# Spreading two of five expert blocks' scores by DMA and weighing them on GpSimd

## The chip, the cores and the metric

The kernel runs on one core of one Trainium2 chip. The metric is the device time of one execution in microseconds; the median of several executions is compared. Matmuls run on TensorE (PE), elementwise work on VectorE (DVE), ScalarE (ACT) and GpSimd (POOL); SyncE (SP) issues DMAs.

## What is computed

64 images of 64x64 pixels with 3 channels go through a Fourier tower of four layers (a small forward transform, a mix of the modes, an inverse transform, a 1x1 convolution, GELU) and a head of two layers, which leaves one 64x64 image each. These are read as 64 sequences of 64 tokens with 64 features, 4096 tokens in all. Then come a retention block, and a layer of 64 experts of which each token uses the best 6. The last is what the change is about:

```python
logits = jnp.einsum('bsd,ed->bse', x, gate_w)
top_logits, indices = jax.lax.top_k(logits, TOP_K)
scores = jax.nn.softmax(top_logits, axis=-1)
W_sel = lattice_weights[indices]
xW = jnp.einsum('bsd,bskde->bske', x, W_sel)
lattice_out = jnp.einsum('bske,bsk->bse', xW, scores)
proj = jnp.einsum('bsd,ed->bse', lattice_out, out_w) + out_b
```

The projection is normalised over the features, scaled, and added to the input of the expert layer.

## The kernel before

The kernel has two blocks, `tower` and then `transformer`. The transformer handles the tokens in 4 chunks (CHUNKS) of 1024 tokens (SLOT), and has two stages.

The first, which I call the front of the transformer, follows an order written out by hand in the list `FRONT`: turns (transposes on PE), projections, retention, gate logits. Each step fills one of four PSUM slots of 1024 columns, and ACT or DVE moves it out; a step may start when the slot that it reuses is moved out. The last steps of a chunk are the gate, its top 6 (`rank`, `take`, `softmax` on DVE, `exponent` on ACT), and `s_turn`, which turns the scores so that experts lie on partitions and tokens along the row (`halves_t`, each score split into a rounded part and the rest, 64 + 64 partitions).

The second, the expert stage, computes every expert for every token, and weighs it by its score, which is zero for the experts not chosen. Two experts make a block (64 features each fill the 128 partitions), so there are EB = 32 blocks a chunk and 128 in all. A block N = 32 g + n takes three steps:

- `spread_block` on PE (L1056): two matmuls of 512 columns with a 0/1 matrix `select` copy the two experts' score rows onto 64 partitions each, into one of PB = 3 PSUM slots.
- `weigh_half` on DVE (L1268), twice: spread scores times `y_t`, the turned tokens (doubled to 128 partitions), into one of WB = 4 buffers `weighted`.
- `gather` on PE (L1067): two matmuls in f32 with the experts' weights add the block to a PSUM sum for the chunk.

On PE the spreads of two blocks stand ahead of the gathers of the two before them. When the 32 blocks of a chunk are summed, ACT copies the sum, PE multiplies it with `out_w` (`project`, L1083), and DVE normalises it in nine steps, `finish(g, 0)` to `finish(g, 8)`. These stand between the weighings of the next chunk, one after each second block from n = 8 to n = 24; the last chunk's nine steps end the kernel. GpSimd prepares two sums for each chunk (L1507, L1509), and SP stores the results (L955).

Much scratch lies in the tower's large tile, so the profile calls `y_t`, `weighted`, `h` and others by the name `modes`.

Of the kernel before, what the change touches and what calls it, by code (L numbers as in the profile page):

```python
# [9 lines left out]
F32 = mybir.dt.float32  # L10
# [29 lines left out]
CT = TILES // CHUNKS  # L40
WB = 4
H_STORES = 8 * 16
# [115 lines left out]
class Front:  # L158

    def __init__(self, ctx, nc):  # L160
        self.modes = ctx.enter_context(nc.sbuf_tensor("modes", [128, IMAGES, MODES // 2, 32], F32))
        self.space, self.at = flat(self.modes[:]), 0
        self.h = self.part(TILES, D)
        self.centred_x = self.part(CHUNKS, CT, D)
        self.normed = self.part(CHUNKS, CT, D)
        self.stats_x = self.part(CHUNKS, 3, CT)
        self.w = self.part(3 * D)[0:D]
        self.rope = self.part(4, D)
        self.decay = self.part(128)
        self.y_t = self.part(TOKENS)  # L170
        self.y2 = self.part(TILES, 2, D)
        self.weighted = self.part(WB, SLOT)
# [629 lines left out]
class Steps:  # L802
# [28 lines left out]
    ("qkv", 3, 1), ("y_turn", 1, 0), ("scores", 2, 0), ("gate", 1, 0), ("attend", 2, 0), ("qk_turn", 3, 0),  # L831
    ("qk_turn", 3, 1), ("s_turn", 0, 0), ("scores", 3, 0), ("y_turn", 2, 0), ("attend", 3, 0), ("gate", 2, 0),
    ("s_turn", 1, 0), ("y_turn", 3, 0), ("gate", 3, 0), ("s_turn", 2, 0), ("s_turn", 3, 0)
])
GUARD = 3.0e38
EB = EXPERTS // 2
PB = 3


def transformer(nc, slots, ident, front, h_dram, gate_t, lattice, out_wt, out_b, ln_g, ln_b, k_select, out):  # L840

    with ExitStack() as ctx:
# [8 lines left out]
        w, rope, decay = front.w, front.rope, front.decay  # L851
        y_t, y2, weighted = front.y_t, front.y2, front.weighted
        h_stored, h_in, front_in, x_variance = front.h_stored, front.h_in, front.front_in, front.x_variance
# [6 lines left out]
        turned = sb("at_turned", [128, 2, 2, CT, D])  # L860
        qk_t = weighted[0:D].rearrange("p (b q) n -> p b q n", q=2)
# [43 lines left out]
        weigh = sem("ex_weigh")  # L905
        summed = sem("ex_summed")
        mixed_out = sem("ex_mixed_out")
# [15 lines left out]

        def after_weigh(g, n, half):

            return 2 * (g * EB + n) + half + 1

        @block.sync
        def _(sp):
# [21 lines left out]
            for c in range(2, CHUNKS):  # L951
                load_select(c)
            for g in range(CHUNKS):
                sp.wait_ge(result_set, g + 1)
                sp.dma_start(out.rearrange("(t b) h w -> (b h) t w", b=2)[:, tiles_of(g)],  # L955
                             result[:, g % 2]).then_inc(stored[g % 2], 16)
            for b in range(2):
                sp.wait_ge(stored[b], 16 * CHUNKS // 2)

        @block.tensor  # L960
        def _(pe):
# [85 lines left out]

            def spread_block(g, n):

                for half in range(2):  # L1050
                    N = g * EB + n
                    if N >= PB:

                        pe.wait_ge(weigh, 2 * (N - PB) + half + 1)
                    at = g * SLOT + half * 512
                    nc.tensor.matmul(slots[:, N % PB, half * 512:(half + 1) * 512],  # L1056
                                     select[:, n * 128:(n + 1) * 128], halves_t[:, at:at + 512],
                                     start=True, stop=True).then_inc(spread, 1)

            def gather(g, n):  # L1060

                pe.wait_ge(weigh, after_weigh(g, n, 1))
                if n == 0 and g >= 2:

                    pe.wait_ge(added, g - 1)
                for j in range(2):
                    mm = nc.tensor.matmul(slots[j * D:(j + 1) * D, SLOTS - 1, g % 2 * 512:g % 2 * 512 + 512],  # L1067
                                          lattice_w[:, n, :],
                                          weighted[:, (g * EB + n) % WB, j * 512:(j + 1) * 512],
                                          start=(n == 0), stop=(n == EB - 1))  # L1070
                if n == EB - 1:
                    mm.then_inc(summed, 1)

# [44 lines left out]
            qk_turn(3, 1)  # L1118
            s_turn(0)
            score(3)  # L1120
            y_turn(2)
            attend(3)
            gate(2)
            s_turn(1)
            y_turn(3)
            gate(3)
            s_turn(2)
            s_turn(3)

            pe.wait_ge(weights_in, WEIGHTS)  # L1130
            wait_moved("s_turn", CHUNKS - 1)
# [3 lines left out]
            spread_block(0, 0)  # L1135
            spread_block(0, 1)
            for g in range(CHUNKS):
                for k in range(EB // 2):
                    for n in (2 * k + 2, 2 * k + 3):
                        if n < EB:  # L1140
                            spread_block(g, n)
                        elif g + 1 < CHUNKS:
                            spread_block(g + 1, n - EB)
                    for n in (2 * k, 2 * k + 1):
                        gather(g, n)
                    if k == 1 and g > 0:
                        project(g - 1)
            project(CHUNKS - 1)
# [4 lines left out]
        def _(dve):  # L1153
# [78 lines left out]
            def rank(c):  # L1232

                wait_moved("gate", c)
                for t in range(CT):
                    last = nc.vector.max(top[:, t, :], logits[:, c % 2, t, 0:EXPERTS])  # L1236
                link(last)
                nc.vector.tensor_tensor(level[:, c % 2], logits[:, c % 2, :, 0:EXPERTS], along(top[:, :, 0], EXPERTS),
                                        ALU.subtract).then_inc(shifted, 1)
# [22 lines left out]

            def weigh_half(g, n, half):

                N = g * EB + n
                dve.wait_ge(spread, after_weigh(g, n, half))
                at = g * SLOT + half * 512
                nc.vector.tensor_tensor(weighted[:, N % WB, half * 512:(half + 1) * 512],  # L1268
                                        slots[:, N % PB, half * 512:(half + 1) * 512], y_t[:, at:at + 512],
                                        ALU.mult).then_inc(weigh, 1)  # L1270
# [83 lines left out]
            wait_moved("s_turn", CHUNKS - 1)  # L1354
            for g in range(CHUNKS):
                for n in range(EB):
                    for half in range(2):
                        weigh_half(g, n, half)
                    if g > 0 and n >= 8 and n % 2 == 0 and n // 2 - 4 < 9:
                        finish(g - 1, n // 2 - 4)  # L1360
            for step in range(9):
# [3 lines left out]
        def _(act):  # L1365
# [51 lines left out]
            def move_s(c):  # L1417

                move("s_turn", c, 0, halves_t[:, c * SLOT:(c + 1) * SLOT])

            def round_select(c):

# [41 lines left out]
            round_select(3)  # L1464
            move_s(0)
            double_y(2)
            move_y(2)
            move_gate(2)
            root_y(3)
            move_s(1)  # L1470
            exponent(2)
            double_y(3)
            move_y(3)
            move_gate(3)
            move_s(2)
            exponent(3)
            move_s(3)
            for g in range(CHUNKS):
                act.wait_ge(summed, g + 1)
# [3 lines left out]
                root(nc, stats_o[:]).then_inc(o_root, 1)  # L1483

        @block.gpsimd
        def _(pool):
# [15 lines left out]
            pool.wait_ge(weights_in, WEIGHTS)  # L1502
            for g in range(CHUNKS):
                pool.wait_ge(y_set, g + 1)
                if g >= 2:
# [4 lines left out]
                                        ALU.add).then_inc(h_shifted, 1)  # L1510


def build(nc, x, x_turned, fc0, fc0_t, sw, cwt, cb, fc1_w, fc1_b, fc2_w, fc2_b, wqkv, gate_t, lattice,
          out_wt, out_b, ln_g, ln_b, k_fwd_w, k_fwd_h, k_inv_h, k_inv_w, k_lift_mask,
          k_rope, k_decay, k_select,
          k_ident, out):
    h_dram = nc.dram_tensor("h_scratch", (IMAGES, HH, WW), F32, kind="Internal").ap()
    with (
        nc.psum_tensor("slots", [128, SLOTS, SLOT], F32) as slots,
# [8 lines left out]
              k_fwd_w, k_fwd_h, k_inv_h, k_inv_w, k_lift_mask)  # L1528
        transformer(nc, slots, ident, front, h_dram, gate_t, lattice, out_wt, out_b, ln_g, ln_b, k_select, out)

# [54 lines left out]
```

## Time and profile before

| | |
|---|---|
| median of 3 runs | 1771.46 us (1771.33 to 1779.39) |
| profiled execution | 1771.06 us, of which its span is 1769.3 us |
| PE busy | 1631.4 us (92%) |
| DVE busy | 1246.6 us (70%) |
| ACT busy | 581.4 us (33%) |
| POOL busy | 28.9 us (2%) |
| expert stage, first spread to last gather | 1553.4 to 1755.6 us |

The span goes from the first to the last instruction; 1.8 us of the execution lie outside of it. The whole change lies behind 1518 us of the span. A `L` number is a line of the kernel before; an f32 matmul of one line of code appears as two in the profile.

### The profile page before, as it was taken

To read this page: it belongs to the slowest core of one execution; us is meant where nothing else is said; L and a number is where in the kernel's file an instruction comes from. 1 tells how busy PE (TensorE), PEld (TensorE's weight loads), DVE (VectorE), ACT (ScalarE), POOL (GpSimd) and SP (SyncE) were. 2 spreads that over 40 slices of the span, in tenths; PEclk is the share of its full clock that TensorE was granted. 3 is DMA by queue.
4 is the path that set the end of the run, shared out by engine and by line. 5 is a ranking of instruction groups with operands and counts; after the bars stand their busy time and mean duration, and the time that the engine had idled before them with its cause. 6 is when DMAs were issued, how large, how long until landed. Compare 5 with 4: busy or idle time off the path is not lost. (4 is left out here: it accounts for less than half of the span.)

```text
span 1769.3 us, 43294 instructions
## 1 busy us (share of the span) xinstructions
PE 1631.4 (92%) x19696; PEld 949.9 (54%) x19696; DVE 1246.6 (70%) x1500; ACT 581.4 (33%) x779; POOL 28.9 (2%) x21
## 2 busy tenths in 40 slices
PE   7999999989999999899999989999988868699997
PEld 2665555557555555665555548777611128534432
DVE  3398988966898898588988974555300028878887
ACT  2333223223232232132322313444478855300000
POOL 1000000000000000000000000000000003000000
PEclk9999999999999999999999999999999988689998
DMA  5233232245655655456556553999876630000000
GB/s 194 81 139 123 118 144 98 119 182 170 241 208 230 231 209 233 143 215 232 209 229 232 208 206 109 335 359 356 330 272 232 231 113 24 1 1 1 7 6 12
DMA packets 59222, 300.01 MB, mean 170 GB/s; under 512 B 17504, under 2 KB 19488, under 8 KB 25120
## 3 DMA queue, kind: packets, MB, share of 16 engines
q1 hardware_dynamic: 40608, 163.01, 27.0%
q10 hardware_dynamic: 18432, 134.23, 18.4%
q8 instruction: 156, 2.56, 0.6%
q14 instruction: 26, 0.21, 0.0%
HBM read 160.90 MB, written 136.31 MB: 168 GB/s over the span
## 5 line engine op out<-in xcount | busy, mean ns | idle before, releaser
L519 PEld LDWEIGHTS slots<-inv_w,inv_out 128*128 128x128 f32 x4096 | 499.1, 196 | 179.3 <-issue 179.3
L756 ACT ACTIVATE act_c<-slots,conv_b 128x512 f32<-128x512 f32 x512 | 352.2, 688 | 739.6 <-PE slots L519 739.6
L519 PE MATMUL slots<-inv_w,inv_out 128*128 128x128 f32 x4096 | 540.7, 287 | 0.0
L673 DVE STREAM_TRANSPOSE inv_out<-slots 128x1024 f32<-128x1024 f32 x256 | 304.6, 1228 | 98.3 <-PE slots L491 98.3
L649 DVE STREAM_TRANSPOSE turned_h<-slots 128x1024 f32<-128x1024 f32 x200 | 237.9, 1228 | 37.4 <-PE slots L429 37.0
L638 DVE STREAM_TRANSPOSE turned_w<-act_c 128x1024 f32<-128x1024 f32 x192 | 225.2, 1216 | 0.0
L429 PE MATMUL slots<-turned_w,fwd_w 32*64 32x512 f32 x3200 | 202.7, 615 | 17.9 <-DVE turned_h L649 10.4
L1268 DVE TENSOR_TENSOR modes<-slots,modes 128x512 f32<-128x512 f32 x256 | 158.4, 683 | 27.2 <-PE slots L1056 25.7
L767 ACT ACTIVATE inv_out<-slots,b 128x1024 f32<-128x1024 f32 x128 | 135.6, 1110 | 25.1 <-PE slots L599 25.1
L441 PE MATMUL slots<-turned_h,fwd_h 64*64 64x320 f32 x1600 | 138.2, 458 | 4.9 <-DVE modes L655 4.9
L655 DVE STREAM_TRANSPOSE modes<-slots 128x640 f32<-128x640 f32 x96 | 81.4, 847 | 86.5 <-PE slots L441 86.5
L511 PE MATMUL slots<-act_c,conv_w 32*32 32x512 f32 x3072 | 111.7, 604 | 19.9 <-DVE modes L655 15.0
L1067 PE MATMUL slots<-modes,ex_lattice_w 128*64 128x512 f32 x512 | 126.4, 610 | 0.1
L491 PE MATMUL slots<-turned_k,inv_h 32*64 32x320 f32 x2048 | 102.1, 454 | 13.5 <-DVE turned_k L663 7.2
L429 PEld LDWEIGHTS slots<-turned_w,fwd_w 32*64 32x64 f32 x3200 | 60.4, 133 | 86.6 <-issue 68.3
L663 DVE STREAM_TRANSPOSE turned_k<-modes 128x640 f32<-128x640 f32 x128 | 103.1, 808 | 0.1
L599 PE MATMUL slots<-act_c,w 32*64 32x512 f32 x1024 | 73.3, 626 | 22.7 <-ACT inv_out L767 20.2
L478 PE MATMUL slots<-modes,mode_w 64*64 64x128 f32 x1600 | 90.3, 270 | 3.8 <-DVE modes L655 2.9
L478 PEld LDWEIGHTS slots<-modes,mode_w 64*64 64x64 f32 x1600 | 89.3, 132 | 6.2 <-DVE modes L655 4.7
L728 DVE TENSOR_SCALAR turned_h<-slots,b 128x512 f32<-128x512 f32 x4 | 3.0, 751 | 118.4 <-PE slots L610 118.4
L441 PEld LDWEIGHTS slots<-turned_h,fwd_h 64*64 64x64 f32 x1600 | 52.0, 133 | 54.0 <-issue 11.0
L695 DVE COPY modes<-slots 128x640 f32<-128x640 f32 x40 | 33.0, 825 | 67.2 <-PE slots L478 67.2
(121 smaller groups left out, 806.3 us busy)
## 6 DMA issues: line engine op xcount, KB each, us to landing
act_scratch<-act_c ACTq DMA_DIRECT2D x128, 1024.0 KB, 4.8
act_c<-act_scratch SPq DMA_DIRECT2D x128, 1024.0 KB, 5.1
mode_w<-in_sw_dram SPq DMA_DIRECT2D x40, 320.0 KB, 3.0
turned_w<-in_x_turned_dram SPq DMA_DIRECT2D x4, 1024.0 KB, 5.6
xin<-in_x_dram SPq DMA_DIRECT2D x4, 1024.0 KB, 7.5
ex_select_raw<-in_k_select_dram SPq DMA_DIRECT2D x4, 512.0 KB, 4.2
h_scratch<-turned_h SPq DMA_DIRECT2D x32, 32.0 KB, 3.1
modes<-h_scratch SPq DMA_DIRECT2D x8, 128.0 KB, 4.6
```

The lines of the kernel that those rows point to most:

```text
L429: mm = nc.tensor.matmul(banks[i * 64:(i + 1) * 64, 4 + p, :], fwd_w[p * 32:(p + 1) * 32, wh, :], turned_w[p * 32:(p + 1) * 32, n % 2, wh, ...
L441: mm = nc.tensor.matmul(banks[kwh * 64:(kwh + 1) * 64, i, 0:320], fwd_h[i * 64:(i + 1) * 64, parity, ph, :], turned_h[i * 64:(i + 1) * 64, ...
L478: mm = nc.tensor.matmul(mix_sums(rows_b, k)[:, at:at + 128], mode_w[rows_b, n % RING_W, m, :], modes[rows_b, :, k, 2 * m:2 * m + 2], start ...
L511: nc.tensor.matmul(banks[q * 32:(q + 1) * 32, p, :], w, src, start=True, stop=False, skip_group_check=True)
L519: mm = nc.tensor.matmul(banks[:, p, at:at + 128], inv_out[:, t % 2, i, p, :, :, r].rearrange("p b o -> p (b o)"), inv_w[:, i, :], start=Fa ...
L638: last = nc.vector.transpose(dst, src)
L649: nc.vector.transpose(dst, src).then_inc(w_turned, 1)
L673: nc.vector.transpose(dst, src).then_inc(inv_turned, 1)
L756: nc.scalar.activation(act_c[:, t % RING, :, p, :], banks[:, p, :].rearrange("p (i m) -> p i m", i=2), ACT.Gelu, bias=conv_b[:, l:l + 1]). ...
L767: nc.scalar.activation(unit[:, n % 2, a:a + 2, :], banks[:, at:at + 2, :], ACT.Gelu, bias=b1[:, 0:1]).then_inc(unit_set, 1)
L1067: mm = nc.tensor.matmul(slots[j * D:(j + 1) * D, SLOTS - 1, g % 2 * 512:g % 2 * 512 + 512], lattice_w[:, n, :], weighted[:, (g * EB + n) % ...
L1268: nc.vector.tensor_tensor(weighted[:, N % WB, half * 512:(half + 1) * 512], slots[:, N % PB, half * 512:(half + 1) * 512], y_t[:, at:at + ...
```

## The change

Of every five blocks N, those with N % 5 of 1 or 3 are now weighed on GpSimd: 51 of 128. Their scores are not spread by PE. A new turn, `level_turn`, follows each `s_turn` in the front and turns the unsplit scores; ACT moves them into `level_t` (64 partitions, one for each expert), SP stores them into a DRAM tensor `level_dram`, and for each GpSimd block SP loads two of its rows, each repeated onto 64 partitions, into one of six buffers `rows_of` (ROWS_RING) made of front tiles that are free by then. GpSimd multiplies the whole 128x1024 block at once. `weighted` gets six buffers, and a semaphore `gathered` counts the blocks that PE has summed, since both writers must wait for a buffer to be read. The stores of the result move from SP's queue to ACT's.

```diff
-WB = 4
+WB = 6
...
+ROWS_RING = 6
+def on_pool(N):
+
+    return N % 5 in (1, 3)
...
+        weighted = [front.weighted[:, b, :] for b in range(4)]
+        weighted += [flat(qkv[:])[:, 2 * SLOT:3 * SLOT], flat(centred_y[:])]
+        rows_of = [flat(turned[:])[:, 0:SLOT], flat(turned[:])[:, SLOT:2 * SLOT], flat(ret_t[:])[:, 0:SLOT],
+                   flat(ret_t[:])[:, SLOT:2 * SLOT], flat(straight[:]), flat(crossed[:])]
+        level_t = normed_t
...
+            e, n = FRONT.moved_of("attend", CHUNKS - 1)
+            sp.wait_ge(moved[e], n)
+            for c in range(CHUNKS):
+                e, n = FRONT.moved_of("level_turn", c)
+                sp.wait_ge(moved[e], n)
+                sp.dma_start(level_dram[:, c * SLOT:(c + 1) * SLOT], level_t[:, c % 2, :]).then_inc(level_stored[c], 16)
+            for i, N in enumerate(POOL_BLOCKS):
+                g, n = N // EB, N % EB
+                if i >= ROWS_RING:
+                    sp.wait_ge(weigh_pool, i - ROWS_RING + 1)
...
+                sp.wait_ge(level_stored[g], 16)
+                sp.dma_start(rows_of[i % ROWS_RING], level_dram[2 * n:2 * n + 2, g * SLOT:(g + 1) * SLOT].rearrange(
+                    "e (a t) -> e a t", a=1).broadcast_to([2, D, SLOT])).then_inc(rows_in[i % ROWS_RING], 16)
...
+            for N in DVE_BLOCKS[0:2]:
+                spread_block(N)
+            for N in range(BLOCKS):
+                if not on_pool(N) and DVE_BLOCKS.index(N) + 2 < len(DVE_BLOCKS):
+                    spread_block(DVE_BLOCKS[DVE_BLOCKS.index(N) + 2])
+                gather(N)
+                if N % EB == 3 and N > EB:
+                    project(N // EB - 1)
...
+                if half == 0 and N >= WB:
+                    dve.wait_ge(gathered, N - WB + 1)
...
+            for i, N in enumerate(POOL_BLOCKS):
+                g = N // EB
+                pool.wait_ge(rows_in[i % ROWS_RING], 16 * (i // ROWS_RING + 1))
+                if N >= WB:
+                    pool.wait_ge(gathered, N - WB + 1)
...
+                nc.gpsimd.tensor_tensor(weighted[N % WB], rows_of[i % ROWS_RING], y_t[:, g * SLOT:(g + 1) * SLOT],
+                                        ALU.mult).then_inc(weigh_pool, 1)
```

The first place is the end of SP's queue; `ex_vectors` are the last weights. Before:

```order
53 L949 DMA ex_vectors<-in_out_b_dram 128x64
54 L949 DMA ex_vectors<-in_ln_g_dram 128x64
55 L949 DMA ex_vectors<-in_ln_b_dram 128x64
56 L935 DMA ex_select_raw<-in_k_select_dram 128x1024 x2
57 L955 DMA out_dram<-modes 128x8x64 x4
```

And of the change (`at_normed_t` is `level_t`, and the tiles ahead of `<-level_scratch` are the buffers `rows_of`):

```order
55 L972 DMA ex_vectors<-in_ln_b_dram 128x64
56 L958 DMA ex_select_raw<-in_k_select_dram 128x1024 x2
57 L981 DMA level_scratch<-at_normed_t 64x1024 x4
58 L990 DMA at_turned<-level_scratch 128x1x1024 x2
59 L990 DMA at_ret_t<-level_scratch 128x1x1024 x2
60 L990 DMA at_straight<-level_scratch 128x1x1024
61 L990 DMA at_crossed<-level_scratch 128x1x1024
```

The four stores of the result have gone to ACT, and four stores of turned scores and 51 loads of rows stand in their place, the first six of them shown. The shape is that of the destination, 128 partitions by 1024. The source of the loads at L990 counts 2 (the rows), then 64 (the repeats, with a step of zero), then 1024, by the `broadcast_to([2, D, SLOT])` in the diff; every DMA of the kernel before counts 16, 32, 64 or 128 in the outermost dimension of both its sides.

The second place is PE from the last turns into the expert stage. Before:

```order
840 L974 MATMUL slots<-ident,ex_halves 128x128 x16
841 L1056 MATMUL slots<-ex_halves_t,ex_select 128x512 x8
842 L1067 MATMUL slots<-modes,ex_lattice_w 64x512 x4
843 L1056 MATMUL slots<-ex_halves_t,ex_select 128x512 x4
844 L1067 MATMUL slots<-modes,ex_lattice_w 64x512 x4
```

And of the change (L1094 are the spreads, L1109 the gathers; `at_qkv` and `at_centred_y` are the two new buffers of `weighted`):

```order
843 L1007 MATMUL slots<-ident,ex_level 64x128 x8
844 L1007 MATMUL slots<-ident,ex_halves 128x128 x8
845 L1007 MATMUL slots<-ident,ex_level 64x128 x8
846 L1094 MATMUL slots<-ex_halves_t,ex_select 128x512 x6
847 L1109 MATMUL slots<-modes,ex_lattice_w 64x512 x4
848 L1094 MATMUL slots<-ex_halves_t,ex_select 128x512 x2
849 L1109 MATMUL slots<-modes,ex_lattice_w 64x512 x4
850 L1094 MATMUL slots<-ex_halves_t,ex_select 128x512 x2
851 L1109 MATMUL slots<-at_qkv,ex_lattice_w 64x512 x2
```

Each of the last two turns is followed by one of `level`, and the second gather of row 847 is already that of block 1, which GpSimd weighs.

The third place is ACT in the same stretch of the front. Before:

```order
301 L1375 CAST ex_halves_t<-slots 128x1024
302 L1402 COPY modes<-modes 128x8x64
303 L1375 COPY modes<-slots 128x1024
304 L1375 COPY ex_logits<-slots 128x8x64
305 L783 ACTIVATE at_stats_y<-at_stats_y 128x8
306 L1375 CAST ex_halves_t<-slots 128x1024
307 L1415 ACT_TABLE_LOAD
308 L1415 ACTIVATE ex_level<-ex_level 128x512
```

And of the change, where the copies into `at_normed_t` are those of the new turns:

```order
301 L1419 CAST ex_halves_t<-slots 128x1024
302 L1419 COPY at_normed_t<-slots 64x1024
303 L1446 COPY modes<-modes 128x8x64
304 L1419 COPY modes<-slots 128x1024
305 L1419 COPY ex_logits<-slots 128x8x64
306 L783 ACTIVATE at_stats_y<-at_stats_y 128x8
307 L1419 CAST ex_halves_t<-slots 128x1024
308 L1419 COPY at_normed_t<-slots 64x1024
309 L1459 ACT_TABLE_LOAD
310 L1459 ACTIVATE ex_level<-ex_level 128x512
```

One new copy stands ahead of the doubling of y (L1402, now L1446), which PE's next turn of y waits for, and one ahead of an exponential (L1415, now L1459).

## Rows read from the trace of the kernel before

**Rows 1.** The page: span, busy time of each engine, TensorE's granted clock in 40 slices.

```profile
span 1769.3 us, 43294 instructions
PE 1631.4 (92%) x19696; PEld 949.9 (54%) x19696; DVE 1246.6 (70%) x1500; ACT 581.4 (33%) x779; POOL 28.9 (2%) x21
PEclk9999999999999999999999999999999988689998
```

**Rows 2.** The chain that ended last, expert stage: start us, us, what.

```profile
1608.71 1.87 PE slots L1067 x8
1610.57 1.04 PE slots L1083 x8
...
1612.77 1.12 PE slots L1056 x4
1613.89 1.87 PE slots L1067 x8
...
1641.14 1.99 PE slots L1067 x8
...
1647.48 1.87 PE slots L1067 x8
...
1751.99 3.61 PE slots L1067 x16
```

**Rows 3.** The timeline where the expert stage starts: start us, us, engine, line.

```profile
1550.34 1.94 PE L974 MATMUL slots<-ident,ex_halves 128*128 128x128 f32 x8 [6.37 <-DVE ex_halves L1261]
1552.32 1.01 ACT L1375 CAST ex_halves_t<-slots 128x1024 fp32r<-128x1024 f32 x1 [6.77 <-PE slots L974]
1553.43 3.75 PE L1056 MATMUL slots<-ex_halves_t,ex_select 128*128 128x512 f32 x8 [1.15 <-issue]
1557.11 2.58 PE L1067 MATMUL slots<-modes,ex_lattice_w 128*64 128x512 f32 x8
```

**Rows 4.** The timeline of the front's end, ACT and PE.

```profile
1520.98 0.62 ACT L1402 COPY modes<-modes 128x512 f32<-128x512 f32 x1
1532.79 1.28 ACT L1415 ACT_TABLE_LOAD   x1
1535.43 1.94 PE L974 MATMUL slots<-ident,modes 128*128 128x128 f32 x8 [3.70 <-ACT modes L1402]
```

**Rows 5.** Groups of instructions from 1450 us on: turns of 64 features, their copies.

```profile
L974 PE MATMUL slots<-ident,at_turned 128*64 128x128 f32 x64 | 11.4, 347 | 0.2 <-DVE at_turned L1204 0.2
L1375 ACT COPY at_normed_t<-slots 64x1024 f32<-64x1024 f32 x4 | 4.0, 1005 | 5.0 <-PE slots L974 5.0
```

**Rows 6.** Stretches: busy us of each engine, granted clock, DMA share, GB/s.

```profile
1272.00:1276.00 4.00, 2.48 (x44) 1.59 (x44) 0.00 (x0) 0.75 (x2) 0.00 (x0) 1.00 1.01 418
1644.00:1648.00 4.00, 3.98 (x18) 1.37 (x18) 4.00 (x7) 0.00 (x0) 2.50 (x2) 1.00 0.32 70
```

**Rows 7.** DMA: a queue's packets, MB, share; two issues with KB, us to landing.

```profile
q1 hardware_dynamic: 40608, 163.01, 27.0%
ex_select_raw<-in_k_select_dram SPq DMA_DIRECT2D x4, 512.0 KB, 4.2
out_dram<-modes SPq DMA_DIRECT2D x4, 256.0 KB, 2.6
```

**Rows 8.** The timeline where GpSimd and DVE work together in the expert stage.

```profile
1643.93 8.46 DVE L1268 TENSOR_TENSOR modes<-slots,modes 128x512 f32<-128x512 f32 x14
1643.99 1.27 POOL L1507 TENSOR_TENSOR modes<-modes,ex_vectors 128x512 f32<-128x512 f32 x1 [136.57 <-DVEq L1305]
```

**Rows 9.** The timeline of the front: small DVE operations beside GpSimd, and one alone.

```profile
1466.14 2.49 POOL L1497 TENSOR_TENSOR at_straight<-at_qkv,modes 128x512 f32<-128x512 f32 x2 [2.21 <-ACT at_qkv L1375]
1466.23 1.20 DVE L790 TENSOR_TENSOR modes<-modes 128x8 f32<-128x8 f32 x1
...
1480.39 0.17 DVE L790 TENSOR_TENSOR at_stats_y<-at_stats_y 128x8 f32<-128x8 f32 x1
```

**Rows 10.** The timeline of the kernel's end.

```profile
1756.26 2.26 PE L1083 MATMUL slots<-ex_out_w,at_qkv 64*128 64x64 f32 x16 [0.69 <-ACT at_qkv L1480]
...
1758.55 0.69 DVE L1279 TENSOR_TENSOR modes<-slots,modes 128x512 f32<-128x512 f32 x1 [4.65 <-PE slots L1083]
...
1766.25 0.37 SPq L955 DMA_DIRECT2D out_dram<-modes  x1
```

More of the change, by code:

```diff
@@ L837, with transformer @@
 PB = 3
-def transformer(nc, slots, ident, front, h_dram, gate_t, lattice, out_wt, out_b, ln_g, ln_b, k_select, out):
+BLOCKS = CHUNKS * EB
+ROWS_RING = 6
+def on_pool(N):
+    return N % 5 in (1, 3)
+POOL_BLOCKS = [N for N in range(BLOCKS) if on_pool(N)]
+DVE_BLOCKS = [N for N in range(BLOCKS) if not on_pool(N)]
+def transformer(nc, slots, ident, front, h_dram, level_dram, gate_t, lattice, out_wt, out_b, ln_g, ln_b, k_select, out):
     with ExitStack() as ctx:
@@ L905, in transformer @@
         weigh = sem("ex_weigh")
-        summed = sem("ex_summed")
+        weigh_pool = sem("ex_weigh_pool")
+        gathered = sem("ex_gathered")
+        level_stored = [sem(f"ex_level_stored{c}") for c in range(CHUNKS)]
+        rows_in = [sem(f"ex_rows_in{b}") for b in range(ROWS_RING)]
         mixed_out = sem("ex_mixed_out")
@@ L952, in _ @@
                 load_select(c)
[L953 to L958, printed above, removed]
+            e, n = FRONT.moved_of("attend", CHUNKS - 1)
[8 more added lines that the diff above has]
+                    sp.wait_ge(weigh_pool, i - ROWS_RING + 1)
+                else:
+                    e, m = FRONT.moved_of("qk_turn", CHUNKS - 1, 1)
+                    sp.wait_ge(moved[e], m)
+                sp.wait_ge(level_stored[g], 16)
+                sp.dma_start(rows_of[i % ROWS_RING], level_dram[2 * n:2 * n + 2, g * SLOT:(g + 1) * SLOT].rearrange(
+                    "e (a t) -> e a t", a=1).broadcast_to([2, D, SLOT])).then_inc(rows_in[i % ROWS_RING], 16)
         @block.tensor
@@ L1119, in _ @@
             s_turn(0)
+            level_turn(0)
             score(3)
@@ L1124, in _ @@
             s_turn(1)
+            level_turn(1)
             y_turn(3)
@@ L1127, in _ @@
             s_turn(2)
+            level_turn(2)
             s_turn(3)
+            level_turn(3)
             pe.wait_ge(weights_in, WEIGHTS)
-            wait_moved("s_turn", CHUNKS - 1)
+            wait_moved("level_turn", CHUNKS - 1)
             wait_moved("attend", CHUNKS - 1)
@@ L1134, in _ @@
             pe.wait_ge(lattice_in, 16)
[L1135 to L1147, printed above, removed]
+            for N in DVE_BLOCKS[0:2]:
[6 more added lines that the diff above has]
+                    project(N // EB - 1)
             project(CHUNKS - 1)
@@ L1237, in rank @@
                 link(last)
+                if c >= 2:
+                    dve.wait_ge(filled, FRONT.filled_at("level_turn", c - 2))
                 nc.vector.tensor_tensor(level[:, c % 2], logits[:, c % 2, :, 0:EXPERTS], along(top[:, :, 0], EXPERTS),
@@ L1354, in _ @@
             wait_moved("s_turn", CHUNKS - 1)
-            for g in range(CHUNKS):
-                for n in range(EB):
+            for N in range(BLOCKS):
+                g, n = N // EB, N % EB
+                if not on_pool(N):
                     for half in range(2):
-                        weigh_half(g, n, half)
-                    if g > 0 and n >= 8 and n % 2 == 0 and n // 2 - 4 < 9:
-                        finish(g - 1, n // 2 - 4)
+                        weigh_half(N, half)
+                if g > 0 and n >= 8 and n % 2 == 0 and n // 2 - 4 < 9:
+                    finish(g - 1, n // 2 - 4)
             for step in range(9):
@@ L1419, in move_s, with move_level @@
                 move("s_turn", c, 0, halves_t[:, c * SLOT:(c + 1) * SLOT])
+            def move_level(c):
+                if c >= 2:
+                    act.wait_ge(level_stored[c - 2], 16)
+                move("level_turn", c, 0, level_t[:, c % 2, :], rows=D)
             def round_select(c):
@@ L1483, in _ @@
                 root(nc, stats_o[:]).then_inc(o_root, 1)
+                act.wait_ge(result_set, g + 1)
+                act.dma_start(out.rearrange("(t b) h w -> (b h) t w", b=2)[:, tiles_of(g)],
+                              result[:, g % 2]).then_inc(stored[g % 2], 16)
+            for b in range(2):
+                act.wait_ge(stored[b], 16 * CHUNKS // 2)
         @block.gpsimd
@@ L1502, in _, with shift @@
             pool.wait_ge(weights_in, WEIGHTS)
-            for g in range(CHUNKS):
+            def shift(g):
                 pool.wait_ge(y_set, g + 1)
@@ L1510, in _ @@
                                         ALU.add).then_inc(h_shifted, 1)
+            shift(0)
+            shift(1)
+            e, n = FRONT.moved_of("y_turn", CHUNKS - 1)
+            pool.wait_ge(moved[e], n)
+            for i, N in enumerate(POOL_BLOCKS):
[3 more added lines that the diff above has]
+                    pool.wait_ge(gathered, N - WB + 1)
+                else:
+                    e, n = FRONT.moved_of("scores", CHUNKS - 1)
+                    pool.wait_ge(moved[e], n)
+                nc.gpsimd.tensor_tensor(weighted[N % WB], rows_of[i % ROWS_RING], y_t[:, g * SLOT:(g + 1) * SLOT],
+                                        ALU.mult).then_inc(weigh_pool, 1)
+                if g >= 1 and N % EB in (28, 29) and g + 1 < CHUNKS and (i + 1 == len(POOL_BLOCKS) or POOL_BLOCKS[i + 1] > g * EB + 29):
+                    shift(g + 1)
 def build(nc, x, x_turned, fc0, fc0_t, sw, cwt, cb, fc1_w, fc1_b, fc2_w, fc2_b, wqkv, gate_t, lattice,
@@ L1528, in build @@
               k_fwd_w, k_fwd_h, k_inv_h, k_inv_w, k_lift_mask)
-        transformer(nc, slots, ident, front, h_dram, gate_t, lattice, out_wt, out_b, ln_g, ln_b, k_select, out)
+        transformer(nc, slots, ident, front, h_dram, level_dram, gate_t, lattice, out_wt, out_b, ln_g, ln_b, k_select, out)
 def kernel(**inputs):
```

60 lines of the change are left out of this document (36 added, 24 removed).

## The prediction, made before the changed kernel ran

> **What bounds the kernel now.** I read the page first. PE is busy for 92% of the span, DVE for 70%, and POOL for 2% [rows 1]; all that the change touches lies in the last six of the 40 slices, where the clock row reads 6, 8, 9, 9, 9, 8 tenths [rows 1]. Then I read the chain of work that ended last, in the expert stage. It is PE and nothing else: 1.87 us for the gathers of two blocks (eight records), 1.12 us for the spreads of two blocks (four), so 2.99 us for two blocks, of which 0.56 us a block is spreading and 0.935 us gathering [rows 2]. A projection puts 2.19 us between two pairs (1608.71 to 1613.89 is 5.18 us) [rows 2]. While `finish` runs on DVE, pairs take a little longer (1.99 for 1.87 us) [rows 2], about 2 us over the three windows. So PE bounds the stage, DVE is close behind, and fewer spreads would be real time, if what replaces them keeps up. That is the question for the rest: something else must deliver a block's spread scores as fast as PE consumes blocks.
>
> **What the change removes.** 51 blocks lose their spread: 51 x 0.56 = 28.6 us of PE [rows 2]. Per five blocks PE's work falls from 7.48 us to 5 x 0.935 + 3 x 0.56 = 6.36 us. DVE loses 51 weighings of two halves, at 8.46 / 14 = 0.604 us a half [rows 8].
>
> **What it adds in the front.** A turn of 64 features takes PE 11.4 / 8 = 1.4 us (64 records are eight turns), its copy on ACT 1.0 us [rows 5]. The first copy stands ahead of the doubling of y (1520.98), which PE waits for: 1.0 us. The second stands ahead of the table load (1532.79), the exponential and the next doubling, which the turn of y at 1535.43 waits for, after 3.70 us idle [rows 4]: its own turn of 1.4 us on PE is hidden in that idle time, but it ends only then, and ACT gets the copy done about 1.4 us later than it was free before. The third delays the last exponential, mostly under `take` on DVE; I take 0.5 us. The fourth is on the path: the spreads of the expert stage wait for its copy, 1.4 us after that of the last `s_turn`. Together 4.3 us; it could be 1.4 (only the last) or 4 x 2.4 = 9.6. The copy that releases the stage ended at 1552.32 + 1.01 = 1553.3 [rows 3] and now ends at 1557.6. Call that T0.
>
> **What it adds in the expert stage.** GpSimd multiplies 51 blocks of 128x1024. The trace has only 128x512, 1.27 us [rows 8]; twice that is 2.54 us for a block, 1.27 if length cost nothing. I take 2.54, the cost by element. Two in 6.36 us fit.
>
> The scores come by 51 loads of 128 x 4 KB = 512 KB. Two readings of the rows:
>
> - All 16 DMA engines share a load. The nearest row is `select`, with the same destination shape: 512 KB landed 4.2 us after its issue [rows 7]. At most one load in 3.18 us is needed, and six may be in flight. Hidden, but for the first.
> - The load is dealt out by its outermost dimension. The destination has 128 there, but the source has two rows. Then only two engines work, each on one row's 64 copies. The fastest stretch moved 418 GB/s at a share of 1.01 of 16 engines [rows 6], 25.9 GB/s for each engine, so 4 KB take 0.158 us, and 64 of them 10.13 us. No stretch of the kernel before shows an engine faster. Loads queue behind one another on the same two engines, so a load lands each 10.13 us, however many are in flight.
>
> The kernel before has no DMA with so few in front, so no row decides. I take the second: every transfer that filled all engines has a multiple of 16 outermost on both sides, and this source is the first for which two equal shares are all that it offers there. GpSimd's 2.54 us fit four times into 10.13, and PE's and DVE's work for two and a half blocks even at half the clock (2.5 x 1.87 + 1.5 x 0.94, the latter from 3.75 us for four blocks' spreads [rows 3], 6.1 us) is below it. So the DMA queue would set the time, and PE would wait for GpSimd at nearly every second block.
>
> The Trainium skill, "DMA: Bandwidth & Descriptors", section "Why a DMA increments its semaphore by 16 and not by 1", says that a DMA runs on the largest number of engines up to 16 that divides the outermost counts (other than 1) of both access patterns, as the instruction carries them. By that rule it is 2 here, and the sum is the one below; with all 16 engines it would be the first rival's. No run here shows it yet: all DMAs so far give 16.
>
> **The sum.** Two issues on SP, about 0.4 us each like the last store's 0.37 [rows 10]: 0.8. The store of the last scores, four packets on each engine, is ahead: 0.6. A 512 KB load on 16 engines has 8 packets of 0.158 = 1.3 us each, so 2.9 of its 4.2 us are not transfer [rows 7]. 51 x 10.13 = 516.6 us of transfer. The last load lands at 1557.6 + 0.8 + 0.6 + 2.9 + 516.6 = 2078.5. GpSimd: 2081.0. The gathers of blocks 126 and 127 at half clock, 2 x 1.87: 2084.8. From the last gather to the end it was 1769.3 - 1755.6 = 13.7 us, which the change leaves (the last store moves to ACT's queue, which is idle then); I add 1 us for the projection at a lower clock (2.26 us before [rows 10]): 2099.5. Three stores of results now run beside the loads; one takes each engine 0.32 x 4 = 1.28 us [rows 6], 3.8 us in all: 2103.3. Outside of the span lie 1771.06 - 1769.3 = 1.8 us, and the profiled execution stands 0.4 us below the median: **2105 us**. Nothing hides it: the loads start after the front, and no load can start sooner, since SP waits for the last `level_turn` before it issues the first.
>
> **The range if two engines do it.** The transfer is nearly the whole sum. Above: over the whole kernel the queue moved 163.01 MB in 27.0% of 16 x 1769.3 us, 0.192 us for 4 KB [rows 7], so 12.3 us a load and 110 us more, 2215. Below: the packet rate cannot beat the fastest stretch by much; with 1% of it, no front cost but 1.4, no store beside it: 2092; I go to 2080.
>
> **Rivals.**
>
> 1. *All 16 engines share the load, and it becomes faster.* Then T0 is 1557.6, the first row lands 5.6 us later (0.8 + 0.6 + 4.2), GpSimd is done 2.5 later, and PE gets block 1 at 1565.7 with 127 gathers (118.7 us), 74 spreads (41.4) and three projections (6.6) left, and some 2 us to win the clock back (it gathered the first pair in 2.58 us for 1.87 [rows 3]): last gather at 1734.4, 21 us sooner than 1755.6. Against it: DVE and GpSimd get in each other's way. A DVE operation of 0.17 us took 1.20 us beside GpSimd, as long as GpSimd's own [rows 9]; a weighing, whose one input is in PSUM, did not suffer (14 in 8.46 us) and neither did GpSimd (1.27) [rows 8]. A `finish` has ten operations without a PSUM input that could wait: at 60% GpSimd load and half an operation each, 8 x 0.76, and two in a row some 1.3 us each, 8.7 us. In a window of 16 blocks DVE then has 9.6 x 1.21 + 7.2 (a finish takes 1758.55 to 1766.25 less its waits [rows 10]) + 8.7 = 27.5 us against PE's 20.3, less a lead of some 2.7 us: 4.5 us lost, three times, 13.5. Left over: 7.5 us faster, 1764.
> 2. *All 16 engines, and the waits of `finish` decide: slower.* If each of the ten waits for a whole GpSimd operation, 25.4 us, a window has 43.7 - 20.3 - 2.7 = 20.7 us to lose, 62 in three, less 21: 1812. It turns from gain to loss at 7 us a window, a mean wait of 1.1 us. PE's clock could fall with it, as it did where PE waited in the front (8, 8, 6 and 8 tenths [rows 1]).
> 3. *It changes nothing:* between these two, within 0.5%.
>
> **How the numbers follow.** Two engines: 0.83, since the source's shape is plain in the code and the trace has nothing against it, but has nothing for it either. Rival 1: 0.10, its condition being the nearest row's behaviour. Rival 2: 0.04. Rival 3: 0.03. What a measurement can tell from no change is about 0.5%, 9 us; rival 1's 7.5 us lie at that edge, so I split it, 0.08 beyond and 0.02 within. Faster 0.08, same 0.05, slower 0.87. The two-engine range 2080 to 2215 holds nearly all of its 0.83, some 0.8 in all, so it is the range; the other cases lie 270 us below it, and reaching there would say nothing.
>
> **What the profile of the changed kernel would show.** DMA share near 0.13 and some 52 GB/s through the whole stage, where rival 1 has about 165 GB/s; a load landing each 10.1 us and, with six in flight, some 55 to 60 us after its issue; GpSimd busy a quarter of the stage, its idle time ended by the DMA; PE busy between 30 and 60%, idle until GpSimd, at the lower clock for much of it; the front 4 us longer. Wrong would be: landings near 4 us; PE's idle time ended by DVE in the windows of `finish`; or DMA engines that at two busy are slower than at sixteen (a share above 0.13 with less moved).

## The result

The changed kernel took 2099.06 us (median of four runs, 2092.48 to 2108.69), the kernel before 1771.39 us (four runs): a ratio of 1.185 (95% interval 1.180 to 1.190). I had forecast 2105 us, in a range from 2080 to 2215. The profiled execution took 2092.48 us, of which 2090.7 us are its span.

The page of the changed kernel, whose slices are now 52 us long (L1584 is GpSimd's product, L1109 the gather, L1311 the weighing on DVE):

```profile
span 2090.7 us, 43324 instructions
...
PE 1708.9 (82%) x19626; PEld 942.2 (45%) x19626; DVE 1187.2 (57%) x1398; ACT 584.9 (28%) x783; POOL 148.1 (7%) x72
...
PE   7999999899999899999989998886845555655544
...
PEclk9999999999999999999999999998777765577775
DMA  4332322566565555656528999663011111111110
GB/s 164 125 129 116 131 114 112 175 226 239 207 240 206 192 179 215 236 210 238 225 75 324 350 362 343 229 224 112 21 37 52 52 53 56 52 52 56 52 56 35
...
issue 19%; POOL 6%; DVE 3%; PE 2%; DMA 1%; ACT 1%; POOLq 0%; SPq 0%; DVEq 0%; ACTq 0%
```

The last ten slices are the expert stage. PE, which was busy all the time there before, is now half busy, its granted clock is at 5 to 7 tenths in the mean of a slice, and the DMA row reads 1 (0 in the last slice): two sixteenths of the engines, 52 GB/s. The next view is of a stretch in the middle of the stage: its length, the busy us of PE, of its weight loads, of DVE, ACT and GpSimd, then the clock, the DMA share and GB/s (as in [rows 6]).

```profile
1600.00:1700.00 100.00, 51.39 (x128) 12.22 (x128) 19.12 (x30) 1.87 (x2) 23.38 (x10) 0.72 0.13 52
```

The timeline of SP, GpSimd and PE at the stage's start:

```profile
1551.36 17.48 SPq L990 DMA_DIRECT2D at_ret_t<-level_scratch  x2
...
1562.65 2.34 POOL L1584 TENSOR_TENSOR modes<-at_turned,modes 128x1024 f32<-128x1024 f32 x1 [59.58 <-DMA at_turned<-level_scratch]
...
1565.04 1.98 PE L1109 MATMUL slots<-modes,ex_lattice_w 128*64 128x512 f32 x4 [12.64 <-POOL modes L1584]
...
1582.78 2.34 POOL L1584 TENSOR_TENSOR modes<-at_ret_t,modes 128x1024 f32<-128x1024 f32 x1 [7.76 <-DMA at_ret_t<-level_scratch]
...
1585.17 1.88 PE L1109 MATMUL slots<-modes,ex_lattice_w 128*64 128x512 f32 x4 [4.13 <-POOL modes L1584]
...
1592.87 2.34 POOL L1584 TENSOR_TENSOR modes<-at_ret_t,modes 128x1024 f32<-128x1024 f32 x1 [7.75 <-DMA at_ret_t<-level_scratch]
```

The whole chain stands here: GpSimd waits 7.75 us for a DMA, works for 2.34 us, and then PE, which had waited for GpSimd, gathers. From one product to the next it is 10.09 us (1582.78 to 1592.87). The stage ended like this:

```profile
2069.16 2.34 POOL L1584 TENSOR_TENSOR modes<-at_ret_t,modes 128x1024 f32<-128x1024 f32 x1 [7.74 <-DMA at_ret_t<-level_scratch]
...
2071.55 3.68 PE L1109 MATMUL slots<-modes,ex_lattice_w 128*64 128x512 f32 x8 [4.08 <-POOL modes L1584]
...
2075.28 0.59 ACT L1534 COPY at_qkv<-slots 128x512 f32<-128x512 f32 x1 [69.89 <-PE slots L1109]
...
2075.91 3.99 PE L1123 MATMUL slots<-ex_out_w,at_qkv 64*128 64x64 f32 x16 [0.69 <-ACT at_qkv L1534]
...
2087.64 0.38 ACTq L1539 DMA_DIRECT2D out_dram<-modes  x1
```

All 51 products start between 1562.65 and 2069.16, 50 steps of 10.13 us on average.

A share of 0.13 could also be sixteen engines that are each busy an eighth of the time. But by the start and the duration of every packet of 4 KB between the first and the last product, exactly two packets were under way during 95% of the time, each for 0.16 us (median). In the run with four rows (e2, below) it was four during 88% of the time, and in the run with two loads a block (e1) the most frequent count was 16 (27%). So the queue was served two packets at a time for the whole of the stage.

### The profile page after: what moved, and what is told of

It is laid out like the page before. It is cut to its first block and busy times, and to the rows that moved or that the text cites. A ratio compares the mean times of both kernels' runs of the same rounds, so it can differ in the third digit from the quotient of the medians.

```text
span 2090.7 us, 43324 instructions
## 1 busy us (share of the span) xinstructions
PE 1708.9 (82%) x19626; PEld 942.2 (45%) x19626; DVE 1187.2 (57%) x1398; ACT 584.9 (28%) x783; POOL 148.1 (7%) x72
## 5 line engine op out<-in xcount | busy, mean ns | idle before, releaser
L1109 PE MATMUL slots<-modes,ex_lattice_w 128*64 128x512 f32 x344 | 136.3, 885 | 166.6 <-POOL modes L1584 166.3
L1311 DVE TENSOR_TENSOR modes<-slots,modes 128x512 f32<-128x512 f32 x102 | 65.6, 686 | 263.9 <-PE slots L1094 227.9
L1109 PEld LDWEIGHTS slots<-modes,ex_lattice_w 128*64 128x64 f32 x344 | 22.6, 180 | 233.4 <-POOL modes L1584 204.0
L1556 POOL TENSOR_TENSOR at_straight<-at_qkv,modes 128x512 f32<-128x512 f32 x8 | 11.3, 1432 | 1478.6 <-ACT at_qkv L1419 1476.5
```

## The experiments

Eight kernels ran, besides before and the changed one. The diffs show only the lines that matter; the counts of semaphores that go with them are left out. Single executions of one kernel scatter by several us (before: 1763.44 to 1786.49 in the 13 that e1 to e4 are compared with, median 1771.63; the 17 for e5 to e8 have a median of 1772.61), so I also compare inside of the profiles: the **stage**, from the start of the first spread to the start of the last matmul of the last gather, and the **front**, from the issue of the first `select` load to the first spread. Front and stage (us) are from one profile each.

| kernel | front | stage | ratio to before (95%) |
|---|---|---|---|
| before | 105.7 | 201.6 | 1 |
| changed | 103.7 | 524.8 | 1.185 (1.180 to 1.190) |
| e1, two loads a block | 103.3 | 191.1 | 0.9945 (0.991 to 0.998) |
| e2, four rows | 103.6 | 269.5 | 1.036 (one run) |
| e3, front only | 106.8 | 219.9 | 1.0137 (1.0071 to 1.0203) |
| e4, other rows | 103.6 | 525.4 | 1.182 (one run) |
| e5, e1 with spreads in pairs | 107.1 | 182.0 | 0.9901 (0.9867 to 0.9934) |
| e6, front only, pairs | 107.6 | 200.0 | 1.0003 (0.9977 to 1.0029) |
| e7, e5 with finish spaced | 106.2 | 179.9 | 0.9891 (0.9847 to 0.9936) |
| e8, e7 with early rows | 107.1 | 172.4 | 0.983 (0.9795 to 0.9865) |

**e1_two_loads.** Each block's rows are loaded by two DMAs, one row onto 64 partitions each, so 64 stands outermost on both sides. The bytes and the rows of DRAM are the same; GpSimd waits for both loads of its block.

```diff
-                sp.dma_start(rows_of[i % ROWS_RING], level_dram[2 * n:2 * n + 2, g * SLOT:(g + 1) * SLOT].rearrange(
-                    "e (a t) -> e a t", a=1).broadcast_to([2, D, SLOT])).then_inc(rows_in[i % ROWS_RING], 16)
+                for e in range(2):
+                    sp.dma_start(rows_of[i % ROWS_RING][e * D:(e + 1) * D], level_dram[
+                        2 * n + e:2 * n + e + 1, g * SLOT:(g + 1) * SLOT].broadcast_to([D, SLOT])).then_inc(
+                            rows_in[i % ROWS_RING], 16)
```

> Each row load is issued as two loads of one row onto 64 partitions, so that 64 stands outermost on both sides; nothing else changes. Theory (the number of DMA engines is set by the outermost dimension, 2 in the changed kernel): the loads land some 4 us after issue, the rows are no longer waited for after the first, and the time is that of my first rival with what the changed kernel's trace corrects (front 6 us shorter than I had it, a GpSimd block 2.34 us): about 1757 us, 1744 if the finish windows lose nothing on the port, 1800 if each of the ten operations waits for a whole GpSimd operation. Rival theory (64 reads of one 4 KB row of DRAM are slow whoever reads): the pitch stays near 10 us and the time near 2095 us.

Measured: 1763.38 us, ratio 0.9945 (0.991 to 0.998). The change of the loads' shape alone takes 336 us off the changed kernel and makes it a little faster than before (0.55%). The loads land 4.1 us after issue; the DMA list of its profile (KB, us to landing):

```profile
at_turned<-level_scratch SPq DMA_DIRECT2D x36, 256.0 KB, 4.1
```

The theory stands, the rival (repeated reads of a row are slow) falls.

**e4_other_rows.** The loads keep their shape and read 128 different rows, from the tower's scratch.

```diff
-                sp.dma_start(rows_of[i % ROWS_RING], level_dram[2 * n:2 * n + 2, g * SLOT:(g + 1) * SLOT].rearrange(
-                    "e (a t) -> e a t", a=1).broadcast_to([2, D, SLOT])).then_inc(rows_in[i % ROWS_RING], 16)
+                sp.dma_start(rows_of[i % ROWS_RING], act_dram[i % 16:i % 16 + 2, 0:D, 0:SLOT]).then_inc(
+                    rows_in[i % ROWS_RING], 16)
```

> The 51 loads keep their size, their destination and the count of 2 in front, but read 128 different rows of 4 KB out of the tower's scratch tensor instead of two rows 64 times each (the weighed scores are then not those of the model). Theory (engine count): nothing changes, a load each 10.1 us, about 2097 us. Rival theory (repeated reads of one row are slow): loads land much faster, the time falls towards 1760 us.

Measured: 2094.13 us in one run. GpSimd's timeline in its profile has the same step, 10.09 us:

```profile
1574.36 2.34 POOL L1583 TENSOR_TENSOR modes<-at_turned,modes 128x1024 f32<-128x1024 f32 x1 [7.69 <-DMA at_turned<-act_scratch]
1584.45 2.34 POOL L1583 TENSOR_TENSOR modes<-at_ret_t,modes 128x1024 f32<-128x1024 f32 x1 [7.75 <-DMA at_ret_t<-act_scratch]
```

The 128 rows are now distinct and lie in another tensor, and no dimension of the source has a step of zero. So it is neither the repeat nor which rows are read; what is left is the 2 in front.

**e2_four_rows.** The scores lie twice in DRAM (SP stores each chunk two times), and a load's source counts 4, 32, 1024.

```diff
-                sp.dma_start(rows_of[i % ROWS_RING], level_dram[2 * n:2 * n + 2, g * SLOT:(g + 1) * SLOT].rearrange(
-                    "e (a t) -> e a t", a=1).broadcast_to([2, D, SLOT])).then_inc(rows_in[i % ROWS_RING], 16)
+                sp.dma_start(rows_of[i % ROWS_RING], level_dram[2 * n:2 * n + 2, :, g * SLOT:(g + 1) * SLOT].rearrange(
+                    "e r (a t) -> (e r) a t", a=1).broadcast_to([4, D // 2, SLOT])).then_inc(rows_in[i % ROWS_RING], 16)
```

> The scores are stored twice in DRAM, and a load reads four rows (each of two rows twice), each repeated onto 32 partitions: 4 stands outermost in the source. Theory: four engines, 32 packets each, a load each 5.06 us instead of 10.13, so 51 x 5.06 = 258 us less: about 1841 us, DMA share 0.25. Rival theory (one row read over and over is slow): each row is read half as often by each engine; if the row's bank were the limit, the two copies of a row would give about the same factor of two, so this run alone does not part them, but a fixed cost of a load (anything not by engine) would leave 2095 us.

Measured: 1835.99 us in one run. Its GpSimd timeline and a stretch:

```profile
1596.27 2.40 POOL L1586 TENSOR_TENSOR modes<-at_turned,modes 128x1024 f32<-128x1024 f32 x1 [2.69 <-DMA at_turned<-level_scratch]
1601.32 2.38 POOL L1586 TENSOR_TENSOR modes<-at_ret_t,modes 128x1024 f32<-128x1024 f32 x1 [2.64 <-DMA at_ret_t<-level_scratch]
```

```profile
1600.00:1700.00 100.00, 77.05 (x288) 22.98 (x287) 54.05 (x75) 2.66 (x4) 49.62 (x22) 0.97 0.27 106
```

The step is 5.05 us, half of 10.09, and the share of 0.27 and the 106 GB/s are twice 0.13 and 52. With 2 and with 4 in front the time of a load follows the count; in e1 the loads no longer set the step, so it is no third point on that line.

**e3_front_only.** No block goes to GpSimd; the turns, copies and stores stay.

```diff
 def on_pool(N):
 
-    return N % 5 in (1, 3)
+    return False
```

> All 128 blocks go back to PE and DVE; the new turns, their copies and the four stores into DRAM stay, as do six buffers. It prices the additions to the front. My prediction's term: 4.3 us more than before, 1776 us. Rival from the changed kernel's trace (the added turns keep TensorE busy, its clock stays at full rate for several steps): 2 us less than before, 1769 us. The expert stage as before within 1 us, since a pair of blocks has the same work on PE.

Measured: 1793.45 us, ratio 1.0137 (1.0071 to 1.0203), against both of my numbers. The table tells where: the front is 106.8 us, 1 us longer than before, but the stage is 219.9 us, 18 us longer, with the same work on PE. The chain of its profile there:

```profile
1777.73 1.01 PE slots L1112 x4
1778.74 0.67 PE slots L1097 x2
1779.41 1.01 PE slots L1112 x4
1780.42 0.67 PE slots L1097 x2
1781.08 1.01 PE slots L1112 x4
```

One block each 1.67 us, where before had two in 2.99 us (1.50 each) [rows 2]. The change had also altered the order on PE: one block's spread and one gather in turn, where two blocks' spreads and two gathers were. Two blocks spread singly take 1.34 us for 1.12, and gathered singly 2.02 for 1.87 [rows 2]. That is 0.18 us a block, or 0.35 us for each turn from spreads to gathers and back that the pairs save. By the code e3 has 126 such turns and before 63, so this would be 22 us; the stage is 18 us longer.

**e6_front_pairs.** e3, with PE's order as before:

```diff
-                if not on_pool(N) and DVE_BLOCKS.index(N) + 2 < len(DVE_BLOCKS):
-                    spread_block(DVE_BLOCKS[DVE_BLOCKS.index(N) + 2])
+                if not on_pool(N) and DVE_BLOCKS.index(N) % 2 == 0:
+                    for M in DVE_BLOCKS[DVE_BLOCKS.index(N) + 2:DVE_BLOCKS.index(N) + 4]:
+                        spread_block(M)
```

> e3 (all blocks on DVE, new turns in the front) with PE's order in pairs as before. If the order alone made e3 22 us slower than before, this one is within 2 us of before, on the side that the new turns have in the other traces (the front 103.3 to 103.8 us from the load of select to the first spread, 105.7 before): ratio 0.999. If the front's additions cost what I predicted: 4 us more, ratio 1.002. If something else in e3 (six buffers, the wait for gathered on DVE) made it slow: 22 us more.

Measured: ratio 1.0003 (0.9977 to 1.0029), stage 200.0 us. The order alone was e3's loss (219.9 to 200.0 us of the stage, 0.32 us for each of 63 turns). What the front's additions cost lies within 5 us on either side of nothing; my 4.3 is inside that interval, and so is zero.

**e5_pairs.** e1, with that same edit of PE's order.

> The two loads a block of e1, and PE spreads two DVE blocks in one go, as before, so that there is one change from spreads to gathers for each two DVE blocks, not for each. Theory from e1's and e3's traces (a lone spread of two matmuls and the gather behind it take 1.67 us where a block in pairs takes 1.50, 0.18 us for each change more): 38 changes fewer, 6.8 us less than e1, about 1756 us on e1's chip. Rival (those 0.18 us are hidden by the waits for GpSimd and DVE in e1): the same as e1, ratio to before 0.9945.

Measured: ratio 0.9901 (0.9867 to 0.9934). The interval of e1 (0.991 to 0.998) overlaps this one, but the stage fell from 191.1 to 182.0 us: 9.1 us for 37 turns (75 and 38 by the code), 0.25 us each.

**e7_pairs_spaced.** e5, with `finish` spread over a wider window:

```diff
-                if g > 0 and n >= 8 and n % 2 == 0 and n // 2 - 4 < 9:
-                    finish(g - 1, n // 2 - 4)
+                if g > 0 and n in (6, 9, 12, 15, 18, 21, 24, 26, 28):
+                    finish(g - 1, (6, 9, 12, 15, 18, 21, 24, 26, 28).index(n))
```

> e5 with the nine steps of finish after blocks 6, 9, 12, 15, 18, 21, 24, 26 and 28 in place of every second block from 8 to 24. In e1 PE is busy 18.5 of 20 us in each of the three windows, against 20.0 between them. Theory (DVE's finish steps, stretched up to 2.9 us by GpSimd, make PE wait): 3 to 5 us less than e5. Rival (GpSimd, not DVE, is what PE waits for there): no change.

Measured: ratio 0.9891 (0.9847 to 0.9936), not to be told from e5; the stage is 2.1 us shorter in one profile each. The time leaves it open, and a gain of the 3 to 5 us that I expected isn't shown. In the lists of PE's waits, those for DVE add up to 6.1 us in e5's stage and to 3.8 in e7's, so the wider window saved some 2 us of waiting at most. In e1's profile, DVE operations without a PSUM input are stretched while GpSimd works, as the groups of lines from 1605 to 1735 us show (mean ns ahead of the last bar):

```profile
L1313 DVE TENSOR_TENSOR at_qkv<-slots,modes 128x512 f32<-128x512 f32 x16 | 10.3, 685 | 6.5 <-PE slots L1096 6.4
L1342 DVE TENSOR_TENSOR modes<-modes,ex_stats_o 128x512 f32<-128x512 f32 x3 | 4.9, 1631 | 0.0
L1333 DVE TENSOR_TENSOR at_squares<-modes 128x512 f32<-128x512 f32 x3 | 4.8, 1613 | 0.0
...
L789 DVE TENSOR_TENSOR ex_stats_o<-ex_stats_o 128x8 f32<-128x8 f32 x3 | 3.6, 1210 | 0.1
...
L1335 DVE TENSOR_REDUCE ex_stats_o<-at_squares 128x8 f32<-128x512 f32 x3 | 2.0, 675 | 0.0
```

The squares (L1333) took 1.61 us where the last finish of the same profile, with GpSimd idle, has 0.69, the small product (L789) 1.21 us for 0.17; the weighing (PSUM and SBUF, L1313) and the reduction (one input, L1335) took 0.69 and 0.68 us, what they take beside an idle GpSimd. Summed over the ten operations that could wait, it is 7.5 us for one finish. But PE's waits for DVE over the whole stage of e1 come to 5.4 us, as the list of PE's waits has it:

```profile
PE slots L1111 <- POOL modes L1586: 4.8, 1, 4.8
PE slots L1111 <- DVE modes L1313: 4.3, 6, 1.4
...
PE slots L1111 <- DVE at_centred_y L1313: 1.1, 2, 0.6
```

**e8_early_rows.** e7, and the first six blocks' rows are loaded between the stores of the second and the third chunk. PE's 4.8 us of wait for GpSimd in the list above is that for block 1, at the start.

```diff
+            store_level(0)
+            store_level(1)
             for i, N in enumerate(POOL_BLOCKS):
+                if i == ROWS_RING:
+                    store_level(2)
+                    store_level(3)
```

> e7, and SP issues the first six blocks' row loads after the stores of the first two chunks of scores, ahead of the stores of the last two, so that GpSimd has weighed block 1 by the time that PE wants it. In e1 PE waited 4.83 us for it at the start, and had then lost its clock. Theory: 5 to 7 us less than e7. With e5 and e7 as forecast, about 1745 us on e1's chip. Rival (the loads compete with the last stores and GpSimd with the front's DVE operations): 0 to 2 us less.

Measured: 1741.32 us, ratio 0.983 (0.9795 to 0.9865), the fastest kernel here, 1.7% below before. The stage is 172.4 us, 7.5 less than e7's. (The medians lie 12.8 us apart, but e7's profiled execution reached the front 12.0 us later than e8's, and nothing that the two do differently lies ahead of it.) Its timeline shows GpSimd at work on the first two blocks before the front has ended (the first spread is at 1550.29), and PE going from the first gathers on without a wait:

```profile
1533.40 4.83 POOL L1594 TENSOR_TENSOR modes<-at_turned,modes 128x1024 f32<-128x1024 f32 x2 [32.32 <-ACT modes L1429]
...
1550.29 2.42 PE L1103 MATMUL slots<-ex_halves_t,ex_select 128*128 128x512 f32 x8 [1.20 <-issue]
...
1552.63 3.65 PE L1118 MATMUL slots<-modes,ex_lattice_w 128*64 128x512 f32 x16
```

Only part of the 7.5 us is the wait. In e7 PE waited 2.7 us for the first GpSimd block, and after it PE ran at a lower clock for some us. These are the first 20 us of the stage in e7, and then in e8 (columns as above):

```profile
1561.00:1571.00 10.00, 6.96 (x18) 3.31 (x20) 4.88 (x8) 0.27 (x1) 4.12 (x2) 0.67 0.89 208
1571.00:1581.00 10.00, 10.00 (x42) 3.51 (x38) 4.97 (x8) 0.00 (x0) 8.79 (x5) 0.91 1.04 235
```

```profile
1550.00:1560.00 10.00, 9.66 (x40) 3.92 (x40) 7.36 (x12) 0.19 (x1) 5.34 (x3) 1.00 0.73 186
1560.00:1570.00 10.00, 10.00 (x44) 4.05 (x44) 5.79 (x10) 0.00 (x0) 7.95 (x4) 1.00 0.56 160
```

The granted clock was 0.67 and 0.91 in e7 and 1.00 in both stretches of e8. The first eight spread matmuls, which stand ahead of any wait for GpSimd, already took 2.42 us in e8 for 3.75 in e7 (3.75 before, too [rows 3]). That 1.3 us can't come from the wait, and with one profile of each kernel it isn't shown that the early rows brought it.

## Why the prediction was right, and where its terms were off

**The mechanism** is the one that I chose: a load whose source has two rows outermost was served two packets at a time, as by two DMA engines, and its queue set the time of the stage. Three runs hold it: the same bytes with 64 outermost (1763 us), other bytes with 2 outermost (2094 us), 4 outermost (1836 us, half the step). The Trainium skill, "DMA: Bandwidth & Descriptors", section "Why a DMA increments its semaphore by 16 and not by 1", has the largest number up to 16 that divides both outermost counts; the shares of 0.13 and 0.27 agree with its 2 and 4.

**Its size.** I had 10.13 us a load from the fastest stretch of the kernel before [rows 6]; it was 10.09 alone and 10.13 with all that lay between. I added 3.8 us for the stores of results beside the loads: 506.5 us for 50 steps against 50 x 10.09 = 504.5 leave 2.0.

**The steps of the sum, against the profiled span.** T0: 1557.6 forecast, 1549.3 measured. 2.0 of the 8.3 us are a tower that ended sooner in this execution; the other 6.3 are my term for the front, +4.3, where it was 2.0 shorter (103.7 for 105.7). First row landed 13.4 us after T0 for 14.4. GpSimd's block: 2.34 us for 2.54. The gathers of 126 and 127: 3.7 us, as I had it. The end: 15.5 us for 14.7, since the projection took 3.99 us at the lower clock for 2.26. In sum 2103.3 - 8.3 - 1.0 - 3.8 - 0.2 + 0.8 = 2090.8 for 2090.7. So the sum was 12.6 us too high for this execution, nearly all of it in one direction. That the forecast lies only 6 us from the median is in part luck: the profiled execution was the fastest of the four, 6.6 us below their median, where I had put it 0.4 below.

**The signs.** The share of 0.13, the 52 GB/s, GpSimd busy 23% and PE 51% of the stretch at a clock of 0.72 came as I had written. Two did not: the front was not 4 us longer, and a load did not land 55 to 60 us after its issue. The last one's issue began at 2034.8 and its product at 2069.16, 34 us later, since SP's queue held the issue back although its buffer had been free for some 25 us. Four loads were under way at that time, not six; the time did not depend on it.

**The front's term** was the largest error. The copies did go in where I had them, and the last one came 1.5 us behind that of the last `s_turn` (1.4 forecast). But TensorE's clock differed. The stretch with the turn of y(2) and the gate behind it, before and then in the changed kernel:

```profile
1520.00:1530.00 10.00, 8.26 (x39) 8.29 (x40) 8.16 (x14) 2.54 (x4) 0.00 (x0) 0.54 0.00 0
```

```profile
1518.00:1528.00 10.00, 6.36 (x56) 6.12 (x56) 9.45 (x27) 4.25 (x6) 0.00 (x0) 0.96 0.12 27
```

At a clock of 0.96 for 0.54 the turn of y(2) took 1.06 us for 1.94, and the gate 1.98 us for 3.67. The added turn of chunk 0 stands ahead of both, in a stretch in which PE was busy without a break in either kernel. This is not a steady gain: the fronts of the nine profiles with the added turns lie between 103.3 and 107.6 us, before's one at 105.7. I argue from two profiles here and ran nothing that holds the clock still; what raised the clock, and that the clock is the cause of the scatter, is open.

**Rival 1**, which gave 1764 us, came out when its condition was made true (e1, 1763 us). It was right for a partly wrong reason, and that is luck: two errors of 8 to 9 us cancelled. From the first spread to the last gather I had 190.3 us (1734.4 - 1557.6 + 13.5), and it was 191.1 in e1. I had counted PE's work by the block from a chain in which spreads stood in pairs [rows 2], and the diff breaks the pairs up: I saw the order of the instructions and priced only their number. That term was missing, 9.1 us by e5. And I had the loss in the windows of `finish` at 13.5 us, where PE waited 5.4: the stretch of DVE's operations was near my value (7.5 for 8.7 us), so more of it was hidden; by what, DVE's lead or the slack between steps, no run separates.

**Rival 2** (the waits of finish make it slower) is refuted by e1: 5.4 us, not 62. (Its terms 11.6, 7.2 and 25.4 make 44.2 us a window and not 43.7, so the 62 should be 64; it changes nothing.) **Rival 3** (within 0.5%) is not parted from rival 1: e1 is 0.55% below before, with an interval from 0.2 to 0.9%.

## What to carry to other kernels

Read a DMA's access patterns, not only its bytes: with 2 outermost in the source a 512 KB load held the queue for 10.1 us, while its two halves, issued as loads with 64 outermost, landed in 4.1 us each (median) and no longer set the time; a DMA share that sits at a small multiple of one sixteenth is the sign. When a loop is rewritten to take some of its blocks away, keep the grouping on the engine that bounds it, and price the turns between kinds of work as well as the work. And take the first items of a new supply line out from behind the last ones of the stage before: the stage was 7.5 us shorter with it in one profile each, where the grouping was worth 9.1 and the loads' shape 334.

## What the runs showed of the hardware that I had not expected

The issue of a load on SP's queue itself lasts nearly as long as the load when few engines serve it and others are ahead: 9.84 us (median) in the changed kernel, 4.80 us in e2 and 0.57 us in e1. All that stands behind such a DMA on its queue waits too: the two issues from 1551.36 on took 17.48 us, and the next began at 1568.9.

```profile
L990 SPq DMA_DIRECT2D at_ret_t<-level_scratch x17: 4079/9844/16887, 1551.4 to 2034.8; - x17
```

The same two matmuls for a spread and four records for a gather take 1.67 us a block when they alternate by single blocks (e3) and 1.50 us in pairs [rows 2], at the full clock in both, with no wait shown in the chain. A turn from spreads to gathers and back thus costs 0.35 us by the chain, 0.32 by the stages of e3 and e6, and 0.25 by those of e1 and e5. It stands in no row of its own, but inside the times of the matmuls. What TensorE does in that time is not shown.
